# A two-layer graph kernel: the first layer sums scaled x and projects the sums afterwards

## The reference

```python
# layer 0
A = adj + jnp.eye(adj.shape[0], dtype=adj.dtype)
deg = jnp.sum(A, axis=1)
d_inv_sqrt = jax.lax.rsqrt(deg)
A_hat = A * d_inv_sqrt[:, None] * d_inv_sqrt[None, :]
mm_1 = A_hat @ x
x = _layernorm(x + jax.nn.elu(mm_1 @ w), axis=-1)
# layer 1
agg = jnp.matmul(adj, x)
out = jnp.matmul(agg, W.T) + b
x = _layernorm(x + jax.nn.relu(out), axis=-1)
```

## Time and profile before

| what | value |
|---|---|
| median of 3 runs (lowest, highest) | 886.92 us (886.02, 890.53) |
| the profiled execution, its own time | 887.87 us |
| its span | 885.7 us |
| PE matmul busy | 793.4 us, 90% of the span |
| PE weight loads busy (beside the matmuls) | 653.1 us, 74% |
| DVE busy | 740.4 us, 84% |
| ACT busy | 511.9 us, 58% |
| POOL busy | 189.3 us, 21% |
| DMA | 181.71 MB, mean 205 GB/s |

### The profile page before, as it was taken

The page is one execution under the profiler, slowest core; times in us unless marked ns, Lnnn a source line. Parts: engine busy times, 40 slices in busy tenths (PEclk is TensorE's granted clock), DMA queues, the critical chain, the costliest instruction groups (busy, mean ns, idle before and its releaser), DMA issues.

```text
span 885.7 us, 10783 instructions
## 1 busy us (share of the span) xinstructions
PE 793.4 (90%) x3532; PEld 653.1 (74%) x3532; DVE 740.4 (84%) x611; ACT 511.9 (58%) x1132; POOL 189.3 (21%) x181
## 2 busy tenths in 40 slices
PE   0447959599999999899999999999999999999996
PEld 0335748477878888688888888888888888888884
DVE  2368878798989998698998999898989898888963
ACT  2254646465866564368876755756653765455351
POOL 0003341341344520012221101111210322022021
PEclk9967969899999999999999999999999999999998
DMA  9999987697799999879999977989896898997500
GB/s 273 306 307 292 215 156 174 163 248 186 168 268 283 186 225 215 189 185 213 225 211 210 243 207 197 193 218 194 205 245 197 182 249 183 220 219 178 130 24 25
DMA packets 183590, 181.71 MB, mean 205 GB/s; under 512 B 6768, under 2 KB 183536, under 8 KB 183536
## 3 DMA queue, kind: packets, MB, share of 16 engines
q1 hardware_dynamic: 94704, 93.21, 45.7%
q10 hardware_dynamic: 88832, 87.83, 42.6%
HBM read 176.82 MB, written 4.19 MB: 204 GB/s over the span
## 4 chain that ended last, share of the span: by engine, by line
PE 58%; DVE 1%; issue 0%; ACT 0%; POOLq 0%; POOL 0%; DVEq 0%; ACTq 0%
PE acc L972 18%; PE acc L974 18%; PE acc L973 18%; PE proj L931 3%; PE proj L929 1%; PE acc L952 0%; DVE v_lo L684 0%; DVE stats L837 0%; DVE raw L831 0%; PE acc L1004 0%; ACT v_hi L477 0%; ACT normed L610 0%; POOLq L173 0%; DVE mean_var L842 0%; POOL rstd L445 0%
## 5 line engine op out<-in xcount | busy, mean ns | idle before, releaser
L972 PE MATMUL acc<-a_hi,v_hi 128*128 128x512 f32 x1024 | 408.4, 399 | 43.2 <-DVE a_lo L643 27.6
L457 ACT ACTIVATE a_hi<-turned 128x1024 fp32r<-128x1024 f32 x256 | 264.5, 1058 | 277.6 <-PE acc L974 131.3
L973 PE MATMUL acc<-a_lo,v_hi 128*128 128x512 f32 x1024 | 403.4, 394 | 0.0
L974 PE MATMUL acc<-a_hi,v_lo 128*128 128x512 f32 x1024 | 403.1, 394 | 0.0
L643 DVE TENSOR_TENSOR a_lo<-turned,a_hi 128x1024 fp32r<-128x1024 f32 x256 | 313.1, 1258 | 42.8 <-ACT a_hi L457 32.4
L626 DVE STREAM_TRANSPOSE turned<-raw 128x2048 f32<-128x2048 f32 x122 | 280.0, 2302 | 8.5 <-DMA raw<-in_adj_dram 2.4
L972 PEld LDWEIGHTS acc<-a_hi,v_hi 128*128 128x128 f32 x1024 | 195.4, 191 | 87.3 <-issue 30.3
L974 PEld LDWEIGHTS acc<-a_hi,v_lo 128*128 128x128 f32 x1024 | 195.1, 191 | 41.4
L973 PEld LDWEIGHTS acc<-a_lo,v_hi 128*128 128x128 f32 x1024 | 195.3, 191 | 39.9
L467 ACT ACTIVATE acc<-raw 128x256 f32<-128x256 f32 x198 | 73.0, 368 | 23.0 <-DMA raw<-in_adj_dram 21.6
L418 POOL TENSOR_TENSOR raw<-raw,x_row 128x1024 f32<-128x1024 f32 x8 | 22.6, 2830 | 179.7 <-ACT raw L513 179.7
(11 more groups left out here) (69 smaller groups left out, 413.2 us busy)
## 6 DMA issues: line engine op xcount, KB each, us to landing
raw<-in_adj_dram SPq DMA_DIRECT2D x154, 512.0 KB, 9.5
raw<-in_adj_dram ACTq DMA_DIRECT2D x154, 512.0 KB, 10.0
x_row<-in_x_dram SPq DMA_DIRECT2D x64, 128.0 KB, 6.7
out_dram<-normed ACTq DMA_DIRECT2D x28, 128.0 KB, 3.2
held<-in_adj_dram ACTq DMA_DIRECT2D x4, 512.0 KB, 12.7
held<-in_adj_dram SPq DMA_DIRECT2D x4, 512.0 KB, 12.8
partial<-in_adj_dram ACTq DMA_DIRECT2D x2, 512.0 KB, 17.0
partial<-in_adj_dram SPq DMA_DIRECT2D x2, 512.0 KB, 18.5
```

The costliest lines, as they stand in the source:

```text
L457: nc.scalar.activation(a_hi[u % 2][:, part, :], turned[u % 2][:, part, :], ACT.Copy).then_inc(s_hi, 1)
L972: pe.matmul(dst, v_hi[:, k, ch], a_hi[u % 2][:, t, :], start=begin, stop=False)
L973: pe.matmul(dst, v_hi[:, k, ch], a_lo[u % 2][:, t, :], start=False, stop=False)
L974: ins = pe.matmul(dst, v_lo[:, k, ch], a_hi[u % 2][:, t, :], start=False, stop=end)
```

## The change

Layer 0 now sums the scaled x itself and projects the finished sums, as layer 1 does. x is loaded for all 8 row groups of pass A into `x_in`, a tensor that lies on the memory of `v_lo`; `make_y` reads x from there, and `y_low` reads it there and writes the low half over it. `turn_x`, `keep_xt` and `project_x` are gone, with the semaphores `s_xt_mm`, `s_xt` and `s_xw`. `project` is now 8 matmuls for either layer. `load_x` no longer waits for a projection; for groups 4 to 7 it waits until the chunks held in `v_hi`, `v_lo` and `partial` have been turned, that is until `turn(u14)`, since `x_in`'s late half is held1's memory. `make_y` waits for x to be loaded where it waited for the projection.

```diff
+        x_in = nc.alloc_sbuf_tensor_at("x_in", [P, N // P, C], F32, offset=v_at + 4 * (N // P * C))
...
             def load_x(m):
-                if m >= 1 and m <= GROUPS:
-                    sp.wait_ge(s_xw, m)
+                if FAST <= m < GROUPS:
+                    sp.wait_ge(s_turn, max(units_through[n] for n in HOMES))
                 elif m > GROUPS:
                     sp.wait_ge(s_resx, m - GROUPS)
                 for q in range(STRIPES):
-                    sp.dma_start(x_row[B32 * q:B32 * (q + 1), :, :], nodes_part(x, m % GROUPS, q)).then_inc(s_x, 16)
+                    if m < GROUPS:
+                        home = x_in[B32 * q:B32 * (q + 1), tiles(m), :]
+                    else:
+                        home = x_row[B32 * q:B32 * (q + 1), :, :]
+                    sp.dma_start(home, nodes_part(x, m % GROUPS, q)).then_inc(s_x, 16)
...
             def make_y(row):
                 act.wait_ge(s_dinv, row + 1)
-                act.wait_ge(s_xw, row + 1)
+                act.wait_ge(s_x, 64 * (row + 1))
...
-                    ins = nc.scalar.activation(v_hi[:, tiles(row).start + 2 * t, :], proj[:, t, :], ACT.Copy,
+                    k = tiles(row).start + 2 * t
+                    ins = nc.scalar.activation(v_hi[:, k, :], x_in[:, k, :], ACT.Copy,
                                                scale=dinv[:, GT * row + t:GT * row + t + 1])
...
-                if at == (2 if row < FAST else 3):
-                    keep_xt(row)
...
-                    ins = nc.vector.scalar_tensor_tensor(out=v_lo[:, k, :], in0=proj[:, t, :],
+                    ins = nc.vector.scalar_tensor_tensor(out=v_lo[:, k, :], in0=x_in[:, k, :],
...
             def project(a):
                 i, layer = order_of[a], accs[a][2]
                 pe.wait_ge(s_agg, i + 1)
-                if i == 0:
-                    pe.wait_ge(s_v, GROUPS)
-                elif i <= GROUPS:
+                if 0 < i <= GROUPS:
                     pe.wait_ge(s_elu, (GT + 1) * i)
...
+                weights = w_sb if layer == 0 else wt_sb
                 for t in range(GT):
                     for h in range(CH):
-                        nodes = agg[:, h, P * t:P * (t + 1)]
-                        if layer == 0:
-                            ins = pe.transpose(proj[:, t, P * h:P * (h + 1)], nodes, ident[:])
-                        else:
-                            ins = pe.matmul(proj[:, t, :], nodes, wt_sb[:, h, :], start=(h == 0), stop=(h == CH - 1))
+                        ins = pe.matmul(proj[:, t, :], agg[:, h, P * t:P * (t + 1)], weights[:, h, :],
+                                        start=(h == 0), stop=(h == CH - 1))
...
             for n in range(FIRST_B):
                 row, at = divmod(n, PANELS)
-                if row < FAST and at == 2:
-                    turn_x(row)
                 if row < FAST and at == 3:
-                    project_x(row)
                     fold_degrees(row)
...
-                if row >= FAST and at == 2:
-                    turn_x(row)
-                if row >= FAST and at == 3:
-                    project_x(row)
```

More of the change, by code:

```diff
@@ L243, in gnn_two_layers @@
         s_dinv = sem("dinv_ready")
-        s_xt_mm = sem("x_turned")
-        s_xt = sem("xt_ready")
-        s_xw = sem("xw_ready")
         s_vhi = sem("v_hi_ready")
@@ L891, in fold_degrees @@
                 ins.then_inc(s_dmm, 1)
[L893 to L912, removed]
             def project(a):
@@ L917, in project @@
                 pe.wait_ge(s_agg, i + 1)
-                if i == 0:
-                    pe.wait_ge(s_v, GROUPS)
-                elif i <= GROUPS:
+                if 0 < i <= GROUPS:
                     pe.wait_ge(s_elu, (GT + 1) * i)
-                else:
+                elif i > GROUPS:
                     pe.wait_ge(s_res, GROUPS + 2 * (i - 1 - GROUPS) + 1)
+                weights = w_sb if layer == 0 else wt_sb
                 for t in range(GT):
                     for h in range(CH):
-                        nodes = agg[:, h, P * t:P * (t + 1)]
-                        if layer == 0:
-                            ins = pe.transpose(proj[:, t, P * h:P * (h + 1)], nodes, ident[:])
-                        else:
-                            ins = pe.matmul(proj[:, t, :], nodes, wt_sb[:, h, :], start=(h == 0), stop=(h == CH - 1))
+                        ins = pe.matmul(proj[:, t, :], agg[:, h, P * t:P * (t + 1)], weights[:, h, :],
+                                        start=(h == 0), stop=(h == CH - 1))
                 ins.then_inc(s_proj, 1)
```

## The result

The changed kernel takes **900.36 us** (median; 898.43 to 903.29) against 886.83 us for the kernel before on the same chip: ratio 1.0147, 95% interval 1.0107 to 1.0187. It is 13.5 us slower. The forecast was 891.8 us with a range to 897.5: the sign was right, the time lies above the range.

What follows compares the result with a forecast made beforehand. PE bounds passes B and C; in pass A PE and DVE are chains of nearly equal length. 20.6 - 15.7 = +4.9 us on the profiled 887.87 gives 892.8, less 0.95 the forecast 891.8 us; range 886.5 to 897.5.

Steps and rivals of the forecast that it cites:

- passes B and C pay in full: Passes B and C: eight layer-0 projections as multiplications cost 2.58 us more each on a busy PE, +20.6 us.
- The head start of groups 1 to 3: Pass A: degree folds of groups 1, 2 and 3 come 2, 6.5 and 7.5 us earlier.
- the rival that it is lost there: Group 4 of pass A: the 7.5 us head start ends in a DMA wait, 899.3 us; part or whole, chance 0.21.
- its rival: Pass A: PE bounds it throughout, groups 4 to 7 return 17.4 us, total 882.6; wholly or in part, chance 0.14.
- 2.1 from `project_x` alone: Group 1 of pass A: the degree fold, which began behind project_x, can begin 2.1 us earlier.
- that rival: Loads in pass A: transfers were the hidden bound, earlier chunks gain 3 to 5 us, 887 to 889; chance 0.10.
- the Trainium skill's rule that was weighed there: Load queues: spreading DMAs over engines gives no bandwidth, all run on the same 16; letting SP go is worth nothing.
- groups 5 to 7: Pass A up to the last degree sum: DVE regains 3.5 us lost to PE and 1.2 of chunk waits, -4.7.
- make_y and y_low read SBUF instead of PSUM ... I take nothing: Moved reads of make_y and y_low: up to 1.4 us gain or as large a loss, booked as nothing.
- the projection returns whole: Pass A after the last degree sum: DVE waits for gapless PE, so removing group 7's project_x gives -3.5 us.
- The clock rival: Groups 5 to 7: PE's clock falls in three new gaps, losing 5.3 us, up to 897.1 us; chance 0.10.
- the sum's 15.7: Pass A: all returns of groups 1 to 7 and after the last degree sum, 15.7 us back.

Runs made afterwards that it cites:

- the gated kernels: POOL's folding of a chunk waits for DVE's low halves of the last unit before it: changed kernel 898.64 us, with y_low from PSUM too 886.86, kernel before 883.79.
- psum_and_gate: Changed kernel with y_low's first input read from PSUM and POOL's folding waiting for the preceding unit's low halves: 886.86 us, ratio 0.9979.
- Two alterations: Changed kernel with y_low's first input from PSUM (896.05 us), or with POOL's folding waiting for DVE's preceding low halves (898.64 us); both together 886.86 us.
- y_low_from_psum: Changed kernel with y_low's first input read from PSUM (other numbers) instead of x_in in SBUF: 896.05 us, ratio 1.0086.

## Why the prediction was right or wrong

**Right.** The stages were read rightly: passes B and C pay in full (+19.5 in the profile for +20.6; over all runs 540.4 to 543.5 us with the multiplications, 521.1 to 521.9 without). The head start of groups 1 to 3 was 1.8, 4.9 and 7.5 us for 2, 6.5 and 7.5, and in the first two profiles it was carried through group 4 (7.4): the rival that it is lost there fell as a whole. A part of it may hold, as the table below shows. PE was no bound of pass A throughout, as its rival had it, nor did the loads of x bring anything measurable: group 1's fold came 1.6 to 2.8 us earlier for 2.1 from `project_x` alone, without the 3 to 5 of that rival. `load_x(4)` held SP for 9.2 us, forecast 9.1, and no stall came of it. That agrees with the outcome of the Trainium skill's rule that was weighed there (DMA: Bandwidth & Descriptors, Rules for kernel authors). The prediction set the rates of the earlier trace rows against it, 346 GB/s from two queues and 220 from one. They don't contradict it: from 330 to 334 in the same trace both queues share the engines evenly, and the rate is 224 GB/s:

```profile
q10 hardware_dynamic: 443, 0.44, 58.4%
q1 hardware_dynamic: 454, 0.46, 54.2%
```

So it isn't the number of queues that makes the two rates; what does is open.

**The step that failed** is in "groups 5 to 7": "DVE's chain shortens only by what it lost to PE", with the pairs of low halves of 3.25 and 3.43 us booked as such losses, 0.9 and 1.1 us. They were not waits for PE. Each lies beside POOL's L384 to L391, as in the timeline of POOL in the kernel before:

```profile
306.21 1.74 POOL L387 TENSOR_TENSOR normed<-normed 128x320 f32<-128x320 f32 x1
...
318.92 1.75 POOL L387 TENSOR_TENSOR normed<-normed 128x320 f32<-128x320 f32 x1
```

So does every low half of over 1.25 us in pass A, 16 of 86 in the trace before and 21 of 86 in the one after. A long duration of an instruction was read as a wait for another engine, without a look at what ran beside it. The change removed no such overlap. What it costs DVE in pass A, taken as the excess over the gated kernels' low halves, diagonals and a `y_low` in PSUM, was 8.8 us in the profile before and 16.3 in the one after. Before, a good part of that was hidden behind PE: cutting POOL's additions, which shortened DVE's waits for POOL as well, gave 4.9 us there and 12.9 in the change. Up to the last fold groups 5 to 7 returned -0.3 us (7.4 to 7.1) instead of the 4.7 of the sum.

**The second** is "make_y and y_low read SBUF instead of PSUM ... I take nothing". It was weighed by ACT's rows alone, with a bound of 1.4 us. The row that decides was DVE's: 13.2 us became 17.1, and the run with the operand in PSUM was 4.3 us faster. An operation with one operand in PSUM and one in SBUF had become one with two in SBUF.

**The third** is small: "the projection returns whole" behind the last degree sum. From the last fold on 1.7 us came back instead of 3.5 (30.0 to 28.3). The half clock took 0.5 us of that. The rest is DVE's own length: it is busy for 26.88 of those 30.0 us before and for 26.80 of 28.3 after (26.72 of 27.8 at the full clock), so there was little to return before DVE bound this stretch. The clock rival was right in kind, and its 5.3 us too high.

Together: 4.7 + 0.3 in groups 5 to 7 and 1.8 behind the last fold make 6.8 of the 6.9 us by which pass A fell short of the sum's 15.7 (it gave 8.8), and in the pair of kernels with POOL's additions cut it gave 15.6. Less the 1.1 by which passes B and C came out cheaper, that is 5.8, near the 5.6 between the sum's 892.8 for the profiled execution and its 898.43. The other 2.9 us between 891.8 and 900.36 are the places of the two profiled executions: the first lay 0.95 above its median, which the forecast took off, and the second 1.9 below.

These tenths belong to two single profiles. The means over all profiles with the same pass A (two old, three new) place the loss a little differently; the end of the wait comes 6.3 us earlier, in line with the medians' 6.4 to 7.8:

| | fold 3 | fold 4 | fold 7 | wait ends |
|---|---|---|---|---|
| old pass A | 159.6 | 218.5 | 333.0 | 363.0 |
| new pass A | 152.4 | 213.0 | 328.6 | 356.7 |
| earlier by | 7.2 | 5.6 | 4.4 | 6.3 |
| forecast | 7.5 | 7.5 | 12.2 | 15.7 |

Of the 9.4 us that are missing, 5.9 lie in groups 5 to 7, 1.6 behind the last fold and some 1.9 up to group 4, the last within the 3 us of a single profile.

The Trainium skill (SBUF — State Buffer, Who interferes with whom) has the rule that was missing from the forecast: a DVE instruction with two inputs in SBUF contends with a GpSimd instruction that reads SBUF, one with at most one such input doesn't (outside DVE's two-port modes), and `tensor_reduce` never. The runs agree in all three: `y_low` at 23.7 us from SBUF and 13.2 from PSUM beside the same additions, low halves at 111 and 101, reductions at 1.21 throughout. By the same page (Summary: rules for kernel authors) the second one to issue "fully blocks" until the first finishes. The rows at 303.30 to 307.76 agree: both engines lose, DVE's pair 2.1 us and POOL's second addition 0.85, because each in turn came later than an instruction of the other.

**Open.** Whether the change also lets more of POOL's additions fall beside the low halves isn't shown: their sums of old and new pass A overlap from profile to profile. No run tells if a part of the head start is lost in group 4. That `psum_and_gate` came out 4 us below its expectation isn't explained: a gate that also keeps POOL off `y_low` wasn't run, since POOL and DVE would wait for each other.

## What to carry to other kernels

Before an operand moves from PSUM to SBUF, count the SBUF inputs of the instruction that reads it: on DVE the second one meets POOL. When the same instruction shows two durations, look first at what ran beside it, before taking it for a wait. And where two engines are of nearly equal length, work taken from one returns only what the other can follow; here one wait on POOL, which kept two engines apart, gave the kernel before 4.5 us, while 34.7 us of PE's work taken out of pass A returned 6 to 8.

## What the runs showed of the hardware

- Low halves (DVE, two inputs of 1024 columns in SBUF): 1.18 us alone, up to 2.62 us beside POOL's additions, and POOL's 320-column addition 0.88 alone, 1.73 beside them. The one that was issued later ended about its own length after the other. `y_low` (256 columns): at most 0.49 us with an input in PSUM, up to 1.80 with both in SBUF. Transposes (2.30) and reductions (1.21) of DVE stayed the same beside them.
- Two alterations that gave 4.3 and 1.7 us alone gave 13.5 together, since each alone moved the overlap onto the other's instruction.
- After 2.64 us of idle, PE's granted clock fell and the stretch from 328 to 332 had 0.57 in the mean, that is 1.2 GHz for most of it, worth 0.5 us. After 2.62 us of idle at the same place in `y_low_from_psum` it stayed at 2.4 GHz.
